# Adding an expert's gate bias on TensorE and gating a tile in one VectorE operation, in a Mamba, mixture-of-experts and linear-attention kernel

## What is computed

```python
h_NM2H = jnp.einsum('md,ndh->nmh', x_MD, Wl1) + bl1[:, None, :]
a_NMH, b_NMH = (h_NM2H[..., :H], h_NM2H[..., H:])
y_NMD = jnp.einsum('nmh,nhd->nmd', jax.nn.silu(a_NMH) * b_NMH, Wl2) + bl2[:, None, :]
```

## Time and profile before

| what | value |
|---|---|
| median of 3 runs | 3098.73 us (3096.38 to 3099.82) |
| the profiled execution | 3098.88 us, span 3097.0 us |
| TensorE busy | 2569.9 us (83%) |
| VectorE busy | 2255.7 us (73%) |
| ScalarE busy | 1777.0 us (57%) |
| GpSimd busy | 1733.8 us (56%) |
| mean granted TensorE clock | 0.924 |

### The profile page before, as it was taken

One profiled execution on the slowest core, in us unless ns is written; L12 is line 12 of the kernel. 1 busy time (PEld: TensorE's weight loads), 2 busy tenths in 40 slices (PEclk: granted clock), 3 DMA queues, 4 the chain that ended last, 5 costly groups with the idle time before them and its releaser, 6 DMA issues. The chain is left out here.

```text
span 3097.0 us, 36581 instructions
## 1 busy us (share of the span) xinstructions
PE 2569.9 (83%) x13286; PEld 1693.4 (55%) x13286; DVE 2255.7 (73%) x2797; ACT 1777.0 (57%) x2734; POOL 1733.8 (56%) x567
## 2 busy tenths in 40 slices
PE   5457788788788798788787787678999999999999
PEld 2233655655565565565565565555555556455554
DVE  8689899899999999999999999964244243342430
ACT  4456587688687677777867867522232232332322
POOL 2899788788888879879978978831010010110000
PEclk9668899899899899899999999887999999999999
DMA  7222343334333324333333333341010010110000
GB/s 267 73 74 68 113 142 110 109 122 141 114 120 116 131 97 148 111 110 116 131 125 122 113 116 129 116 152 42 1 34 24 10 34 0 34 34 0 7 7 7
DMA packets 143590, 272.65 MB, mean 88 GB/s; under 512 B 23031, under 2 KB 94174, under 8 KB 142430
## 3 DMA queue, kind: packets, MB, share of 16 engines
q1 hardware_dynamic: 137310, 254.12, 24.2%
q0 software_dynamic: 6144, 16.79, 1.6%
HBM read 230.75 MB, written 40.11 MB: 87 GB/s over the span
## 5 line engine op out<-in xcount | busy, mean ns | idle before, releaser
L1037 POOL TENSOR_TENSOR hs<-u,bb 128x2048 f32<-128x2048 f32 x256 | 1159.2, 4534 | 237.7 <-PE hT L1255 231.7
L1167 DVE TENSOR_TENSOR_SCAN hs<-dA,hs 128x1024 f32<-128x1024 f32 x512 | 1162.7, 2277 | 88.2 <-POOL hs L1037 45.5
L1255 PE MATMUL hT<-ident,hs 128*128 128x128 f32 x3648 | 576.2, 299 | 358.4 <-DVE held L1179 307.5
L1083 ACT ACTIVATE dA<-dt,cols 128x511 f32<-128x511 f32 x1024 | 661.0, 680 | 299.3 <-DVE hs L1167 294.2
L1255 PEld LDWEIGHTS hT<-ident,hs 128*128 128x128 f32 x3648 | 441.9, 152 | 512.8 <-DVE held L1179 207.0
L1179 DVE SCALAR_TENSOR_TENSOR held<-hT,ct,held 128x512 f32<-128x512 f32 x880 | 609.7, 733 | 26.5 <-PE hT L1255 26.0
L1526 ACT ACTIVATE gl<-bank,cols_sb 128x512 f32<-128x512 f32 x192 | 130.6, 687 | 527.4 <-PE bank L1765 527.2
L1765 PE MATMUL bank<-mT,cms_sb 128*128 128x512 f32 x768 | 362.7, 597 | 10.1 <-ACT mT L1520 8.6
L144 POOL COPY cur<-slot 128x8 uint32 (+1 forms) x8 | 1.5, 188 | 640.1 <-DVE held L156 628.4
L1274 PEld LDWEIGHTS moe<-xgT,held 128*128 128x128 f32 x2272 | 293.0, 207 | 53.7 <-issue 27.7
L1274 PE MATMUL moe<-xgT,held 128*128 128x128 f32 x2272 | 306.2, 292 | 12.3 <-ACT xgT L1098 12.0
(11 more groups left out here) (228 smaller groups left out, 3248.7 us busy)
## 6 DMA issues: line engine op xcount, KB each, us to landing
held<-wl SPq DMA_DIRECT2D x71, 1024.0 KB
bb<-b_scratch SPq DMA_DIRECT2D x128, 512.0 KB, 5.1
held<-wl SPq DMA_DIRECT2D x71, 512.0 KB
xg<-xg_scratch SPq DMA_DIRECT2D x71, 128.0 KB
yg_scratch<-yg SPq DMA_DIRECT2D x71, 128.0 KB, 1.7
held<-x SPq DMA_DIRECT2D x16, 512.0 KB, 6.4
xg_scratch<-zero SPq DMA_DIRECT2D x8, 1024.0 KB, 6.8
cb<-b_scratch SPq DMA_DIRECT2D x28, 256.0 KB, 5.8
```

The lines of the kernel that those rows point to most:

```text
L1037: nc.gpsimd.tensor_tensor(hs[n % HS][:, :, :], u[d][:, :, :], row, ALU.mult).then_inc(dBu_ready, 1)
L1083: last = nc.scalar.activation(dst, src, ACT.Exp, scale=cols[:, at:at + 1])
L1167: nc.vector.tensor_tensor_scan(h, decay, h, 0.0, ALU.mult, ALU.add).then_inc(scan_done, 1)
L1255: last = nc.tensor.transpose(hT[c % 2][:, k * P:(k + 1) * P], hs[n % HS][:, k, c * P:(c + 1) * P], ident[:, :])
```

## The change

The gated half's bias moves from VectorE to TensorE. Ahead of the eight products of piece b, TensorE issues one product of the identity with `b1`, read with a step of zero over the 128 rows, so that all 512 columns of the bank `moe` start from the bias. The eight products that follow accumulate onto it. VectorE's gate becomes one multiplication of 128x512 elements. Piece a, the SiLU, the down piece, all loads and the order of every engine's stream are as they were; the waits are at the same places.

```diff
                     dve.wait_ge(sa_ready, t + 1)
                     dve.wait_ge(b_ps, t + 1)
-                    for m in range(HB):
-                        last = nc.vector.scalar_tensor_tensor(out=sa[:, m, :], in0=moe[:, m * P:(m + 1) * P],
-                                                              scalar=b1[r][:, HB + m:HB + m + 1], in1=sa[:, m, :],
-                                                              op0=ALU.add, op1=ALU.mult)
-                    last.then_inc(hE_ready, 1)
+                    nc.vector.tensor_tensor(sa[:, :, :], moe[:, :].rearrange("p (m t) -> p m t", t=P), sa[:, :, :], ALU.mult)\
+                      .then_inc(hE_ready, 1)
...
                         at = 0 if piece == "a" else HB
+
+                        if piece == "b":
+                            mm(moe[:, :].rearrange("p (m t) -> p m t", t=P), ident[:, :],
+                               b1[r][:, at:at + HB].rearrange("p (m a) -> p m a", a=1).broadcast_to([P, HB, P]),
+                               start=True, stop=False, skip_group_check=True)
                         for m in range(HB):
                             for k in range(KD):
                                 last = mm(moe[:, m * P:(m + 1) * P], w1[r][:, k, (at + m) * P:(at + m + 1) * P], xgT[:, k, :],
-                                          start=(k == 0), stop=(k == KD - 1))
+                                          start=(k == 0 and piece != "b"), stop=(k == KD - 1), skip_group_check=True)
```

## The result

| what | before | changed |
|---|---|---|
| median | 3098.73 us (7 runs) | 3089.44 us (3086.43 to 3091.72, 7 runs) |
| ratio of the medians | | 0.997, 95% interval 0.996 to 0.9979 |
| the profiled execution | 3098.88 us, span 3097.0 us | 3087.13 us, span 3085.4 us |
| mean granted TensorE clock | 0.924 | 0.928 |

The change makes the kernel 9.3 us faster, 0.3%. The forecast was 3092 us with a range from 3077 to 3106. A later series gave the changed kernel 3085.52 us beside 3097.44 us for the kernel before, ratio 0.9958 (0.9941 to 0.9974); the two intervals overlap.

The account below looks back on a forecast made before the run. VectorE was taken as fullest, busy 227.7 of 242.4 us a period, with other engines setting the pace at its waits. Forward units +0.3, backward -4.9, last unit and first tile -2.4 gave -7.0 us: 3092 us, range 3077 to 3106.

Parts of the forecast that it names:

- first batch: The first batch's tile, outside the forward and full backward units: its gate was to gain, -0.4 us.
- The prices: Added product 0.86 us of TensorE at full clock, no extra for the zero step; each gate 0.41 us shorter on VectorE.
- The forward unit, steps 0 to 8: TensorE full; product at step 3 delays the gate, ScalarE, GpSimd and the scan at step 8, by 0.86 us there.
- the ceiling behind it: Forward unit behind step 8: the gate at step 10 recovers 0.41 us, then ScalarE holds the lateness at 0.45 us.
- that scan is about 0.55 late instead of early: Backward unit, steps 3 to 10: product delays the convolution at step 6, then ScalarE and VectorE's scan, 0.55 us.
- Step 28, "zero": Backward unit: in four of six units half clock makes the gate wait 0.4 us and gain 0.4; two gain 0.41.
- Rival 4: Added work keeps TensorE's clock up, piece b at step 28 takes 1.95 us, four more gates gain: 3090 us; chance 0.03.
- The last unit, "all five gain": Gates there start 3.1 to 4.9 us after piece b, so all five gain: -2.0 us.
- Rival 1: VectorE sets the pace throughout, TensorE's idle time hides the product, 53 of 71 gates count: 3077 us; chance 0.20.
- Rival 2: TensorE's product is paid at step 3 of both units, 13 times, later gates absorbed: 3108 us, slower; chance 0.17.
- Rival 3: ScalarE's full stretches also absorb the backward unit's gates at steps 10 and 16: 3097 us, no change; chance 0.13.
- Rival 5: The single gate operation runs slower than its twin, losing the 0.41 us 71 times: about no change; chance 0.04.

Follow-up runs that it names:

- the repeat: The changed kernel, not edited further, measured again in a later series: 3085.52 us beside 3097.44 us for the kernel before, ratio 0.9958.

## Why the prediction came out as it did

**The time.** Forecast -7.0 us from the profiled execution; the profiles show -11.8 and -11.2 us, the medians -9.3 and -11.9. The first result lies in the forecast's own range from 3088 to 3097 us; the repeat, 3085.52, lies below it. Its case, product and gain each on part of the path, is the one that the experiments bear out. That the time came within 3 us is in part luck: the periods gained over twice what was forecast for them, and the last unit and the first tile next to nothing. To the end of the scan stage the first profile and its repeat compare thus:

| term | forecast | first profile | repeat |
|---|---|---|---|
| start of the scan stage | 0 | -1.64 | +0.14 |
| first batch | -0.4 | -0.02 | -0.01 |
| six periods | -4.7 | -11.05 | -11.24 |
| last forward unit | 0 | +0.42 | +0.04 |
| last unit | -2.0 | -0.54 | +0.05 |
| sum | -7.0 | -12.83 | -11.0 |

In the first profile the last stage gives 1.1 us of it back.

**The prices.** The product at 0.86 us at full clock was right to the hundredth; the zero-step operand costs nothing extra. A gate on VectorE's path gives 0.43 to 0.45 us, not 0.41: the new slot is 1304.41 - 1303.83 = 0.58 us, not 0.61 (the rows had given 0.60).

**The forward unit, steps 0 to 8**, was right link by link, and so was the ceiling behind it: the shift stays at +0.47 us from step 11 to step 16, where ScalarE was said to hold it (forecast +0.45). GpSimd's full stretch swallows the gates at steps 16 and 23, as forecast: the shift falls to +0.04 behind the first of them and is back at +0.43 two scans later. What was missing is the batch's end, +0.50 us a period. Forecast +0.04 a forward unit, measured +0.26.

**The backward unit, "that scan is about 0.55 late instead of early"**, is the step that failed. I had put the product at step 3 on the path, through the convolution at step 6 and ScalarE. It isn't there. With the product alone the scans stay where they are from step 4 to step 10 (+0.01 to +0.02 us in all six units). In the changed kernel the gate at step 4 takes 0.42 us off, 0.32 of it go at step 7, and -0.09 are left at step 10 in the mean; with the gate alone it is the same. So ScalarE's decay blocks take that gain and not the product. To be laid beside the earlier trace rows, where L398 waited 0.31 us for L363, in the changed kernel:

```profile
1458.67 1.94 PE L363 MATMUL prep<-xpad,taps 128*64 128x512 f32 x8
...
1460.76 0.68 ACT L398 ACTIVATE xc<-prep,cols 128x512 f32<-128x512 f32 x1
...
1460.86 2.29 DVE L1167 TENSOR_TENSOR_SCAN hs<-dA,hs 128x1024 f32<-128x1024 f32 x1 [0.23 <-ACT dA L1083]
```

L398 waits for nothing here, where 0.9 us was expected, and the scan waits for `dA`. The rest is the clock's second place: -0.60 us at step 3 and +0.35 at step 4. In two of the six units the latter is the 0.52 us that come back where the half-clock stretch is gone. In three others it is 0.31 to 0.37; the kernel with the old form in the backward units alone has 0.38 and 0.39 in two such units, so that isn't the product's either, but what it is stays open. Net -0.17 us, and that is 4.3 us over six units, the largest part of the miss.

**Step 28, "zero"**, failed too. I took piece b at its 3.62 us and added the product to it. In three units the product instead took the slow stretch on itself; in the other three the transposes ahead were faster, which covered it. Each gate at step 29 gains 0.44 us, in all six units and not in two. Rival 4 had priced just this, at 3090 us, which is the nearest of all to the medians, though gains and losses of the clock at the two other places stand beside it; I gave it 0.03 because the idleness before step 28 isn't filled. It isn't, and the low clock before piece b is still there in three units (the transposes at 1297.70 take 1.94 us). What I overlooked is that a product ahead of piece b can itself be the work behind which the clock comes back. The Trainium skill (TensorE: Matmul & The Clock Gate, Part 1) says that activity releases the throttle; the trace agrees here in three units, with b at 1.95 us behind the product, and 3.62 us without it in the earlier trace rows. In the other three b is still slow behind it, at 2.95 to 3.06 us.

**The last unit, "all five gain"**, failed: -0.5 and 0.0 us in place of -2.0. The gates weren't delayed by TensorE and their gain was there up to step 21, but it didn't reach the unit's end. VectorE's wait of 1.41 us for transposes at half clock takes most of it (1.5 of the 2.3 us that are lost there), and the other 0.8 go by the next scan. The sum had no such term. What takes the gain of the first batch's tile stays open.

**The rivals.** Rival 1 (VectorE everywhere, 3077) is refuted by both series, 3089.44 and 3085.52 us; its time is reached, 3076.45 us, only without any product, and there with the clock's help. Rival 2 had the right place and price in the forward units only: in the backward ones no cost of the product is seen behind step 3. And it fell because the gates at steps 10 and 16 of the backward unit pass through, -0.88 us. Without the shorter gates the product alone does cost 17.7 us, which is rival 2 and more, though 0.89 us a period of it is the clock at the batch's end. Rival 3 is refuted by the same -0.88. Rival 5 is refuted by the group of L1188.

**What stays open.** How the 9 to 12 us split between gates and clock can't be read off exactly, since each edit changes both. At the two places of a period where the scans single the clock out it nearly cancels in the changed kernel: +0.50 us at the batch's end, -0.60 at the backward unit's step 3, of which 0.17 comes back at step 4. The -0.22 us between steps 12 and 28 of the forward unit and the -0.26 between steps 17 and 20 of the backward unit have no account. Single places aren't resolved in time. And why the half-clock stretches fall where they do in a given period isn't settled; the two profiles of the changed kernel have them at the same places, and every edit here moved some of them.

## What to carry to other kernels

Where several engines share the path, price a moved operation at each place in turn: a cheap product at a place where its engine is full costs its whole duration, a saved one only counts up to the next full stretch of another engine. Try to take the worst places out of such a change before giving it up or accepting it whole: here the old form at two of ten tiles, together with idle products that move the half-clock stretches, brought 7 us more than the change alone. What the old form brought by itself, and what the idle products did, isn't separated in time. And when TensorE runs at half clock in front of a wait, any edit of its stream moves the clock as well; repeat the profile, compare the scans step by step, and don't read a 3 us difference as the edit's own price.

## What the runs showed of the hardware that was not expected

- Idle products made the kernel before 3.7 us faster (interval 0.6 to 6.8 us): the same two groups went from 3.04 and 2.61 us to 1.98 and 1.95 us behind them.
- The half-clock stretches fell at the same places in two profiled executions of the changed kernel: the six periods' gains repeat within 0.12 us, though they differ among themselves by 2.4 us. That every execution does so isn't shown; the ten runs with the convolution later spread over 13 us.
- Where the half-clock stretch at the backward unit's steps 1 and 2 is gone, VectorE gains up to 1.67 us there and mostly gives 0.52 us back at the next scan, with and without the change.
- A second added product in 71 tiles, 61 us of TensorE's time by 0.86 us each, made the kernel only 3 to 9 us slower.
- One SiLU of 128x512 from PSUM takes ScalarE 597 ns in the mean. VectorE's multiplication of the same size takes 666 ns.
